# Projecting un-normalised rows with column-centred weights in the second stage of a one-core perceiver kernel

## The reference

```python
x = x + _L0_xattn_ref(ctx_1024, _layernorm(x, axis=-1))   # scores ctx @ x^T, softmax over x's 128 rows, times ctx
x = x + _L0_attn_ref(_layernorm(x, axis=-1), w_attn, b_attn, w_proj, b_proj)  # 16 heads of 16, causal
x = x + _L0_ffn_ref(_layernorm(x, axis=-1), W, b, V_r, C)  # x @ W.T + b + (x @ V_r) @ C.T
def _layernorm(x, axis=-1, eps=1e-05):
    m = jnp.mean(x, axis=axis, keepdims=True)
    v = jnp.var(x, axis=axis, keepdims=True)
    return (x - m) / jnp.sqrt(v + eps)
```

## Time and profile before

| what | value |
|---|---|
| median of three runs | 105.86 us |
| the profiled execution's own time | 105.76 us |
| its span in the profile | 103.7 us |
| PE busy | 98.3 us (95%) |
| DVE, ACT, POOL busy | 76.3, 72.7, 63.8 us |
| DMA traffic | 27.86 MB |

### The profile page before, as it was taken

How to read it: one execution, slowest core, us unless ns; L and a number is a source line. 1 busy time by engine, 2 the same in 40 slices (tenths; PEclk the granted TensorE clock), 3 DMA queues, 4 the chain that set the end, 5 groups by cost and what they waited for, 6 DMA issues and landing times.

```text
span 103.7 us, 2257 instructions
## 1 busy us (share of the span) xinstructions
PE 98.3 (95%) x740; PEld 86.4 (83%) x740; DVE 76.3 (74%) x217; ACT 72.7 (70%) x268; POOL 63.8 (62%) x46
## 2 busy tenths in 40 slices
PE   5999999999999999999999999999999999969990
PEld 1389999999999999999999999999998976845660
DVE  0412959959999999988777797777889745699641
ACT  4019599599999999997777977778879304489410
POOL 6405499869999999999766797666886001004020
PEclk9999999999999999999999999999999999999999
DMA  3899999999999999999999999993000000000001
GB/s 70 330 417 412 411 411 406 408 408 408 414 400 409 403 416 406 408 409 409 408 406 406 411 408 409 388 369 125 0 0 6 0 0 0 0 0 0 6 0 51
DMA packets 8746, 27.86 MB, mean 269 GB/s; under 512 B 1120, under 2 KB 1824, under 8 KB 8736
## 3 DMA queue, kind: packets, MB, share of 16 engines
q1 hardware_dynamic: 8736, 27.73, 68.3%
HBM read 27.59 MB, written 0.13 MB: 267 GB/s over the span
## 4 chain that ended last, share of the span: by engine, by line
PE 89%; DVE 4%; DMA 2%; issue 1%; POOL 1%; ACT 0%; DVEq 0%
PE bank L323 43%; PE bank L335 21%; PE bank L338 10%; DVE head_max L716 2%; DMA x<-x_dram 2%; PE bank L406 2%; PE bank L443 1%; PE bank L344 1%; PE bank L419 1%; PE bank L500 1%; PE bank L308 1%; PE bank L486 1%; PE bank L389 1%; PE bank L386 1%; PE bank L462 1%
## 5 line engine op out<-in xcount | busy, mean ns | idle before, releaser
L288 POOL TENSOR_TENSOR rows_split<-rows_ring,rows_split 128x1024 fp32r<-128x1024 f32 (+1 forms) x25 | 58.4, 2335 | 16.9 <-ACT rows_split L518 16.8
L323 PE MATMUL bank<-query_t,cols_ring 128*128 128x128 f32 x392 | 47.5, 276 | 0.0
L323 PEld LDWEIGHTS bank<-query_t,cols_ring 128*128 128x128 f32 x392 | 45.7, 192 | 1.3 <-ACT query_t L509 0.3
L529 ACT ACTIVATE bank<-bank,neg_max 128x128 f32<-128x128 f32 x98 | 33.1, 338 | 7.4 <-DVE neg_max L653 7.2
L335 PE MATMUL bank<-rows_split,probs 128*128 128x512 f32 x92 | 34.7, 413 | 0.0
L518 ACT CAST rows_split<-rows_ring 128x1024 fp32r<-128x1024 f32 (+1 forms) x25 | 25.8, 1033 | 6.1 <-DMA rows_ring<-ctx_rows_dram 5.1
L670 DVE SCALAR_TENSOR_TENSOR probs<-bank,inv_sums,probs 128x128 fp32r<-128x128 f32 x98 | 27.6, 345 | 0.9
L338 PE MATMUL bank<-rows_split,probs 128*128 128x256 f32 x92 | 25.6, 279 | 0.0
L653 DVE TENSOR_REDUCE neg_max<-bank 128x4 f32<-128x512 f32 (+1 forms) x25 | 16.8, 672 | 8.6 <-PE bank L323 8.6
L335 PEld LDWEIGHTS bank<-rows_split,probs 128*128 128x128 f32 x92 | 17.3, 189 | 3.1
L529 ACT ACTIVATION_READ_ACCUMULATOR bank<-bank,neg_max 128x1 f32 x98 | 19.8, 202 | 0.0
(11 more groups left out here) (96 smaller groups left out, 64.0 us busy)
## 6 DMA issues: line engine op xcount, KB each, us to landing
cols_ring<-ctx_cols_dram SPq DMA_DIRECT2D x24, 512.0 KB, 14.8
rows_ring<-ctx_rows_dram SPq DMA_DIRECT2D x24, 512.0 KB, 15.2
wqk_sb<-w_qk_dram SPq DMA_DIRECT2D x1, 512.0 KB, 11.6
cols_ring<-ctx_cols_dram SPq DMA_DIRECT2D x1, 256.0 KB, 11.3
rows_ring<-ctx_rows_dram SPq DMA_DIRECT2D x1, 256.0 KB, 12.1
wv_sb<-w_v_dram SPq DMA_DIRECT2D x1, 256.0 KB, 11.7
wproj_sb<-w_proj_dram SPq DMA_DIRECT2D x1, 256.0 KB, 10.4
wffn_sb<-w_ffn_dram SPq DMA_DIRECT2D x1, 256.0 KB, 9.7
```

Of the source, the lines that this page charges most:

```text
L288: pool.tensor_tensor(rows_split[:, b, 0:n, 1, :], rows_ring[:, slot * STEP:slot * STEP + n, :], rows_split[:, b, 0:n, 0, :].bitcast(F32), ...
L323: last = pe.matmul(into[:, t * P:(t + 1) * P], cols_ring[:, slot * STEP + t, c, :], query_t[:, c, :], start=(c == 0), stop=(c == DC - 1))
L529: last = act.activation(on[:, t * P:(t + 1) * P], on[:, t * P:(t + 1) * P], ACT.Exp, bias=neg_max[:, b, t:t + 1], accum_out=sums[:, b, t:t ...
```

## The change

The second layer norm is taken apart. With mean m and reciprocal deviation r per row, `layernorm(x1) @ w` equals `r * (x1 @ w')` where every column of each weight's projected dimension has its mean over the 256 inputs subtracted in w'. So x1 itself is turned and projected, and r is multiplied in afterwards. For that:

- A transposed copy of the weights (`w_t`, 0.79 MB) is loaded within the loop, and `w_qk` and `w_v` too instead of after it. DVE sums its rows in steps 10 to 12 (`sum_columns`). The six times 128 negated means go to DRAM by a DMA on ACT's queue after step 14 and come back, spread over all partitions, by another one after step 16, which waits for the first to land. POOL adds them to the weights (`centre_weights`): four parts after steps 20 to 23, two after the loop.
- DVE adds x1 by halves; PE turns each half at once. r is spread along columns by a matmul of ones with a diagonal of r. Keys and queries are copied raw by ACT, multiplied by the spread r on DVE (`scaled`), then finished: the even masks of keys and q0 on ACT, the odd masks on POOL, q1 on DVE.
- v's copy becomes four instructions that multiply by r and add the bias.
- PE does the low rank product alone, one half before and one after the turns; POOL adds it to `wffn_sb`. POOL also takes the addition of x1 and the projection bias. The two masks of scores (`mask_scores`) come after the projections.

```diff
@@ sync: within the loop over s @@
+                if s == WT_AT:                      # 11
+                    sp.dma_start(wt_sb[:], w_t).then_inc(wt_landed, 16)
+                if s == WT_AT + 2:
+                    sp.dma_start(wqk_sb[:], w_qk).then_inc(wqkv_landed, 16)
+                if s == WT_AT + 4:
+                    sp.dma_start(wv_sb[:], w_v).then_inc(wqkv_landed, 16)
@@ gpsimd @@
+            def centre_weights(n):
+
+                pool.wait_ge(means_landed, 16)
+                pool.wait_ge(wqkv_landed, 32)
+                part = wqk_sb[:, :, n, :] if n < 2 * DC else wv_sb[:, :, (n - 2 * DC) * P:(n - 2 * DC + 1) * P]
+                pool.tensor_tensor(part, part, means_wide[:, n, :].unsqueeze(1).to_broadcast([P, DC, P]),
+                                   ALU.add).then_inc(wqkv_centred, 1)
...
+                if CENTRE_AT <= s < CENTRE_AT + CENTRED:   # 20 to 23
+                    centre_weights(s - CENTRE_AT)
+            for n in range(CENTRED, 3 * DC):
+                centre_weights(n)
...
             inverse_std(1)
+            pool.wait_ge(diag_ready, 1)
+            pool.tensor_tensor(x1_bias[:], x1[:], bproj_sb[:], ALU.add).then_inc(x1_bias_ready, 1)
+            for c in range(DC):
+
+                pool.wait_ge(scaled_ready, 2 * c + 1)
+                pool.tensor_scalar(k_t[:, c, 1, :], scaled[:, DC + c, :], bqk_sb[:, DC + c:DC + c + 1], parity[:, 1:2],
+                                   ALU.add, ALU.mult).then_inc(k_copied[c], 1)
+            pool.wait_ge(low_rank_copied, 1)
+            pool.tensor_tensor(wffn_sb[:].rearrange("p c o -> p (c o)"), wffn_sb[:].rearrange("p c o -> p (c o)"),
+                               low_rank[:], ALU.add).then_inc(wffn_ready, 1)
@@ tensor @@
+            multiply_low_rank(0)
             for c in range(DC):
...
+                pe.wait_ge(x1_ready, c + 1)
+                pe.transpose(turn[c][:, 0:P], x1[:, c * P:(c + 1) * P], ident[:]).then_inc(turned, 1)
+            multiply_low_rank(1).then_inc(low_rank_ready, 1)
+            pe.wait_ge(wqkv_centred, 3 * DC)
             pe.wait_ge(turn_copied_first, 2)
...
             for n in [DC, 0, DC + 1, 1]:
+                if n == DC + 1:
+
+                    pe.wait_ge(diag_ready, 1)
+                    pe.wait_ge(ones_ready, 1)
+                    pe.wait_ge(raw_copied, 1)
+                    pe.matmul(rstd_wide_ps, ones[:], rstd_diag[:], start=True, stop=True).then_inc(rstd_spread, 1)
@@ scalar: within the loop, after exponents(s) @@
+                if s == STORE_AT:                   # 14
+                    act.wait_ge(neg_means_ready, 1)
+                    act.dma_start(col_means.rearrange("o (n p) -> p (o n)", p=P), neg_means[:],
+                                  allow_slow_non_contiguous=True).then_inc(means_stored, 16)
+                if s == STORE_AT + 2:
+                    act.wait_ge(means_stored, 16)
+                    act.dma_start(means_wide[:].rearrange("p n d -> p (n d)"), col_means.to_broadcast([P, 3 * D]))\
+                       .then_inc(means_landed, 16)
@@ vector: x1 and what follows @@
-            dve.tensor_tensor(x1[:], weighted_end[:, 0:D], x0[:], ALU.add).then_inc(x1_ready, 1)
-            dve.wait_ge(x1_ready, 1)
-            layer_norm(1, x1[:])
...
+                dve.tensor_tensor(x1[:, half], weighted_end[:, half], x0[:, half], ALU.add).then_inc(x1_ready, 1)
+            dve.wait_ge(x1_ready, DC)
+            statistics(x1[:])
+            dve.wait_ge(rstd_ready, 2)
+            dve.tensor_scalar(rstd_diag[:], ident[:], rstd[:, 0:1], None, ALU.mult).then_inc(diag_ready, 1)
+            dve.wait_ge(rstd_spread, 1)
+            for i, n in enumerate([DC, 0, DC + 1, 1]):
+
+                dve.wait_ge(raw_copied, i + 1)
+                dve.tensor_tensor(scaled[:, n, :], raw[:, n, :], rstd_wide_ps, ALU.mult).then_inc(scaled_ready, 1)
...
+                for c in range(DC):
+                    dve.scalar_tensor_tensor(v_pad[:, c, e, :, e * HD:(e + 1) * HD], v_view[:, c, e], rstd[:, 0:1],
+                                             bv_view[:, c, e], ALU.mult, ALU.add).then_inc(v_copied, 1)
```

More of the change, by code:

```diff
@@ L32 @@
 ENDING = 2
+WT_AT = 11
+SUMS_AT = 10
+STORE_AT = 14
+CENTRE_AT = 20
+CENTRED = 4
 def perceiver_kernel(nc, x, ctx_rows, ctx_cols, w_qk, b_qk, w_v, b_v, w_proj, b_proj,
-                     w_ffn, b_ffn, v_r, c_t, out):
+                     w_ffn, b_ffn, v_r, c_t, w_t, col_means, out):
     T, D = x.shape
@@ L104, in perceiver_kernel @@
         ct_sb = sb("ct_sb", [R, D])
+        wt_sb = sb("wt_sb", [P, 3 * DC, D])
+        col_sums = sb("col_sums", [P, 3 * DC])
+        neg_means = sb("neg_means", [P, 3 * DC])
+        means_wide = sb("means_wide", [P, 3 * DC, P])
+        ones = sb("ones", [P, P])
+        rstd_diag = sb("rstd_diag", [P, P])
+        raw = sb("raw", [P, 2 * DC, P])
+        scaled = sb("scaled", [P, 2 * DC, P])
+        bk_parity = sb("bk_parity", [P, DC, 2])
+        low_rank = sb("low_rank", [P, DC * D])
         q_t = sb("q_t", [P, DC, P])
@@ L554, in _, with copy_keys, copy_queries, finish_keys @@
             copy_turn(1, normed_t)
+            act.wait_ge(turned, 2 * DC)
+            act.copy(normed_t[:, 1, :], turn[1][:, 0:P]).then_inc(turn_copied, 1)
             act.wait_ge(low_rank_ready, 1)
-            act.copy(wffn_sb[:].rearrange("p c o -> p (c o)"), low_rank_ps[:]).then_inc(wffn_ready, 1)
+            act.copy(low_rank[:], low_rank_ps[:]).then_inc(low_rank_copied, 1)
+            def copy_keys(c):
+                act.wait_ge(k_ready, c + 1)
+                act.copy(raw[:, DC + c, :], k_ps[c][:, 0:P]).then_inc(raw_copied, 1)
+            def copy_queries(c):
+                act.wait_ge(q_ready, c + 1)
+                act.copy(raw[:, c, :], q_ps[c][:, 0:P]).then_inc(raw_copied, 1)
+            def finish_keys(c):
+                act.wait_ge(scaled_ready, 2 * c + 1)
+                act.activation(k_t[:, c, 0, :], scaled[:, DC + c, :], ACT.Identity, bias=bk_parity[:, c, 0:1],
+                               scale=parity[:, 0:1]).then_inc(k_copied[c], 1)
+            copy_keys(0)
+            copy_queries(0)
+            copy_keys(1)
+            act.wait_ge(bk_parity_ready, 1)
+            finish_keys(0)
+            act.wait_ge(scaled_ready, 2)
+            act.wait_ge(bq_scaled_ready, 1)
+            act.activation(q_t[:, 0, :], scaled[:, 0, :], ACT.Identity, bias=bq_scaled[:, 0:1], scale=SCALE)\
+               .then_inc(q_copied[0], 1)
+            copy_queries(1)
+            finish_keys(1)
             act.wait_ge(x1_bias_ready, 1)
@@ L612, in link, with statistics @@
                 dve.wait_ge(dve_step, link_count[0])
-            def layer_norm(n, src):
+            def statistics(src):
                 link(dve.bn_stats(bn[:, 0:6], src))
                 dve.bn_aggr(mean_var[:], bn[:]).then_inc(stats_ready, 1)
[L617 to L629, removed]
             dve.memset(warm[:], 0.0).then_inc(warm_ready, 1)
+            dve.memset(ones[:], 1.0).then_inc(ones_ready, 1)
             dve.memset(bn[:, 6:8], 0.0).then_inc(eps_ready, 1)
@@ L636, in _ @@
             dve.wait_ge(x_landed, 16)
-            layer_norm(0, x0[:])
-            copy_turn(0, query_t)
+            statistics(x0[:])
+            dve.wait_ge(stats_ready, 1)
+            dve.wait_ge(rstd_ready, 1)
+            for c in range(DC):
+                half = slice(c * P, (c + 1) * P)
+                dve.tensor_scalar(normed[:, half], x0[:, half], mean_var[:, 0:1], rstd[:, 0:1],
+                                  ALU.subtract, ALU.mult).then_inc(normed_ready, 1)
+            dve.wait_ge(turned, DC)
+            dve.tensor_copy(query_t[:, 1, :], turn[1][:, 0:P]).then_inc(turn_copied, 1)
             def invert(s):
@@ L692, in _ @@
             dve.wait_ge(summed, STEPS)
-            dve.tensor_tensor(x1[:], weighted_end[:, 0:D], x0[:], ALU.add).then_inc(x1_ready, 1)
-            dve.wait_ge(x1_ready, 1)
-            layer_norm(1, x1[:])
-            dve.tensor_tensor(x1_bias[:], x1[:], bproj_sb[:], ALU.add).then_inc(x1_bias_ready, 1)
-            copy_turn(1, normed_t)
-            dve.wait_ge(parity_ready, 1)
-            for c in range(DC):
[L700 to L704, removed]
+            for c in range(DC):
+                half = slice(c * P, (c + 1) * P)
+                dve.tensor_tensor(x1[:, half], weighted_end[:, half], x0[:, half], ALU.add).then_inc(x1_ready, 1)
[7 more added lines that the diff above has]
+                dve.tensor_tensor(scaled[:, n, :], raw[:, n, :], rstd_wide_ps, ALU.mult).then_inc(scaled_ready, 1)
+            dve.wait_ge(scaled_ready, 2 * DC)
+            dve.wait_ge(bq_scaled_ready, 1)
+            dve.tensor_scalar(q_t[:, 1, :], scaled[:, 1, :], SCALE, bq_scaled[:, 1:2], ALU.mult, ALU.add)\
+               .then_inc(q_copied[1], 1)
             def copy_exp_t(j):
```

73 lines of the change are left out of this document (46 added, 27 removed).

## The result

The changed kernel takes 114.0 us (median of 6 runs, 113.41 to 114.25) against 106.1 for the kernel before on the same chip: a ratio of 1.0746 (95% interval 1.0713 to 1.0779). The forecast was 106.3 with a range up to 109.4. Its rival A named the mechanism and put it at 108.7.

A forecast was written before the change was run, and what follows sets the result against it. PE was taken to bound the kernel (89% of the span), so only work between the stages counted: 105.76 + 0.10 (turn) + 0.35 (v's copy) = 106.2, plus 0.10 for the median of runs, 106.3 us; range 105.2 to 109.4.

The forecast's parts named there:

- rival A: Loop: the means' store crawls, 768 4-byte pieces taking turns with SP's packets; landing 9.4, loss 2.4, time 108.7 us; chance 0.33.
- (d): Loop, ACT's store of the means and wait for it: slower by issue plus landing minus 7.4 us; no loss expected.
- near end: Store's landing in the loop taken as 1.7 us, as for the output alone on the engines, not the loads' 14.8.
- break-even of 7.4: Issue plus landing of the means' store, in us, above which the loop was expected to become slower.
- POOL ... catches up nothing: Loop after ACT's wait: POOL, full at 3.2 us a step, hands the whole delay to the last rows part.
- (a) to (c): Loop margins: inserted loads, DVE's sums and POOL's centrings all fit without delaying PE; POOL's last part keeps 2.9 us.
- The turn: Last weighing to end of head scores: 1.5 us won early, given back in later passes; ends 0.1 us later.
- DVE scales q1 to 89.5 and, dependent on that, finishes it to 89.86: Late between the stages: two dependent DVE passes on q1, after which the second half of the head scores starts.
- costed at nothing: Work taken as free because wanted only later, including POOL's 1.29 us wffn addition, ending near 90.6.
- v's copy: After the projections: four 64-column instructions replace two additions on PE's path, 0.84 against 0.48, so +0.35 us.
- Rival B: Between the stages: q1 is ready sooner, second half of head scores ends 0.8 us earlier; time 105.0, chance 0.07.

## Why the prediction was wrong, step by step

**(d), the means through DRAM, is the step that failed.** "ACT's queue has nothing ahead of the store, so I take the near end: no loss." The landing was 17.9, not 1.7, and the store and ACT's wait for it made the last weighing 7.9 late. The near end was a transfer of another shape on engines with nothing else to do; the count of pieces, which I had worked out for rival A, should have set the likeliest value. Having nothing ahead in its own queue did not bring the store near 1.7, since each of its 48 turns per engine waits for a packet of the other queue. From 56 to 58 us of the changed kernel, before the hold, the two queues moved as many packets each:

```profile
DMA packets 433, 0.80 MB, mean 400 GB/s; under 512 B 238, under 2 KB 238, under 8 KB 433
q1 hardware_dynamic: 217, 0.80, 100.1%
q10 hardware_dynamic: 216, 0.00, 6.1%
```

The small packets take hardly any bandwidth (400 GB/s beside them), which is why my argument against rival A (the rate stays at 408 GB/s) was no argument: it looked at what they take, not at how long they wait. The Trainium skill (DMA: Bandwidth & Descriptors, Queues, rings and completion order) has the rule of turns between queues, by whole packets. It held, with one piece to a packet and not the 9 to 17 descriptors that the skill's page calls typical: in the kernel with one piece per partition an engine's 8 pieces were spread over 1.6 us, among SP's packets. Rival A's 9.4 priced the turns nearly right (7.7, measured 8.0 with stretches of their own) and the time before the first piece and behind the last at 1.7; beside the loads it was 4.1, of which 3.9 passed before the first piece moved.

**Rival A's size** was short by these 2.7 and by 5.8 for the hold, which no row before showed. Its break-even of 7.4 was too low, and the two errors partly cancelled: 17.9 - 7.4 would have been a loss of 10.5, not 7.9. By landing the kernels with this store give: 5.6, no late weighing; 12.1, span 2.6 to 3.0 above before, 0.8 of it the turn and v, so about 2 in the loop; 14.2, 88.89 - 84.07 = 4.8; 17.9, 7.9. So it lies nearer to 10. "POOL ... catches up nothing" was the error: its first four rows parts after the wait took 9.48 together, 2.4 each, against PE's 3.18 a step, and only then did its centrings begin. ACT's steps were 2.33 (71.56 - 69.23) and not 2.57, since the rows had landed meanwhile.

**The other margins, (a) to (c), were right**: without the store the last weighing ends at 83.96.

**The turn**: forecast +0.1, measured +0.5. Projections began 93.51 - 91.96 = 1.55 after the last weighing (forecast 1.6), and the first half of the scores at 4.74 (forecast 4.9). The step that was off is "DVE scales q1 to 89.5 and, dependent on that, finishes it to 89.86": it took 0.99 for 0.30, held by the POOL addition that I had costed at nothing because nobody waits for its result. With the collision gone the turn is 0.2 shorter than before (6.27 against 6.46). The Trainium skill says why (SBUF — State Buffer, SBUF: two separate sides): some DVE instructions and any GpSimd instruction share a pair of ports, whichever starts first has it for its whole length, and the other blocks. The trace agrees as far as it goes: DVE's instruction starts behind POOL's and ends at 98.06, where POOL's ends at 97.98; no view shows the ports. DVE's product with the PSUM operand (L806) ran in 0.29 beside the same POOL instruction.

**v's copy**: forecast 0.84, measured 0.85; on the path it cost 0.3.

**Rival B** did not happen, but the turn can gain as it says, with the collision gone and the order on ACT changed: then the kernel stands 0.4% ahead of the one before.

## What to carry to other kernels

Count a DMA's pieces before its bytes: on engines that are full, a piece of 4 bytes waits for as long as a 4 KB packet of the other queue, so lay data out in one run per partition, and do not scatter single words over a small stretch of DRAM. Here one engine's wait for a DMA stopped the others too; work out for which landing the lead is used up, and put the wait where even the far end fits. When work is moved to GpSimd because nobody waits for its result, look at what DVE runs at that time.

## What the hardware showed that was not expected

- 768 writes of 4 bytes to interleaved words in DRAM landed after 10.4 us on idle engines, 7.6 of them after the last packet, and after 17.9 beside loads; to SBUF, or to DRAM 32 bytes apart with each engine in a stretch of its own, 12.1 beside loads. During the hold the loads fell to 84 GB/s. Whether spacing or ownership of the stretch cures it was not separated, and what holds the writes stays open; that neighbouring words fall to different engines follows from the layout and an even split, and no view names a packet's engine.
- After PE had stood idle for 5 us the granted clock was 0.50 (1.2 in place of 2.4 GHz) from 74.4 to 77.1 us, and four tiles of its weighing took 0.64 each against 0.35 later. It cost little here, since the last weighing had to wait for POOL all the same.
- A DVE instruction of 128 columns took 0.99 us beside a GpSimd instruction of 1.27 us and 0.29 without it.
